# Latent attention on one core: four heads of two sequences a step, query rows packed into blocks of 128

## The reference, cut to what matters

```python
def _L0_attn_ref(x, wq_a, q_a_ln_w, wq_b, wkv_a, kv_a_ln_w, wkv_b, wo):
    H, NOPE, ROPE, VD, KVR = 32, 64, 64, 128, 64
    q = _rmsnorm(x @ wq_a.T, q_a_ln_w) @ wq_b.T          # 256 -> 32 heads x 128
    q_nope, q_pe = q[..., :NOPE], q[..., NOPE:]
    ckv, k_pe = split(x @ wkv_a.T)                       # 64 latents + 64 rope, shared by all heads
    k_nope, v = split(_rmsnorm(ckv, kv_a_ln_w) @ wkv_b.T)
    q_pe, k_pe = rope(q_pe), rope(k_pe)
    scores = einsum('bqhd,bkhd->bhqk', [q_nope, q_pe], [k_nope, k_pe]) * softmax_scale
    attn = softmax(where(causal, scores, min))
    return einsum('bhqk,bkhd->bqhd', attn, v) @ wo.T
```

## Time and profile before

| what | value |
|---|---|
| median of 3 runs | 2403.49 us (2399.36 to 2407.38) |
| the profiled execution | 2404.33 us, of which its span is 2402.7 us |
| busy over the span | PE 97%, PEld 85%, DVE 75%, ACT 52%, POOL 51% |
| attention in the span | first scores at 887.6 us, last exp at 1541.0 us |

### The profile page before, as it was taken

One profiled execution on the slowest core, in us unless ns is written; L12 is line 12 of the kernel. 1 busy time (PEld: TensorE's weight loads), 2 busy tenths in 40 slices (PEclk: granted clock), 3 DMA queues, 4 the chain that ended last, 5 costly groups with the idle time before them and its releaser, 6 DMA issues. The chain is left out here.

```text
span 2402.7 us, 45878 instructions
## 1 busy us (share of the span) xinstructions
PE 2321.9 (97%) x14640; PEld 2038.0 (85%) x14640; DVE 1812.4 (75%) x3575; ACT 1241.6 (52%) x3742; POOL 1216.4 (51%) x1012
## 2 busy tenths in 40 slices
PE   8999999998999979999999999899999998999998
PEld 6888888887677758999999999788888887999998
DVE  8987775896577758888988888655786566777775
ACT  5566654552455549999999999623223223111110
POOL 5567786672133347767776776420675553111110
PEclk9999999999999979999999999899999999999999
DMA  7774567779477720111111112296888997111111
GB/s 249 240 230 149 174 226 254 256 248 323 140 228 241 239 87 24 58 53 56 40 56 52 48 48 74 79 332 188 247 249 236 304 279 262 54 71 71 70 70 53
DMA packets 319400, 382.00 MB, mean 159 GB/s; under 512 B 23680, under 2 KB 227968, under 8 KB 319104
## 3 DMA queue, kind: packets, MB, share of 16 engines
q1 hardware_dynamic: 311472, 352.30, 46.2%
q0 software_dynamic: 7184, 25.69, 2.7%
q10 hardware_dynamic: 576, 2.10, 0.3%
HBM read 297.68 MB, written 81.80 MB: 158 GB/s over the span
## 5 line engine op out<-in xcount | busy, mean ns | idle before, releaser
L1547 ACT ACTIVATE attn_prob<-attn_prob,attn_bias 94x94 f32<-94x94 f32 x1024 | 366.8, 361 | 47.3 <-DVE attn_bias L1623 45.9
L682 DVE TENSOR_TENSOR up_t_lo<-early_raw,up_t_hi 128x512 fp32r<-128x512 f32 (+1 forms) x210 | 220.4, 1054 | 102.1 <-ACT up_t_hi L609 99.1
L551 POOL TENSOR_TENSOR early_raw<-early_raw 128x512 f32<-128x512 f32 (+1 forms) x150 | 222.6, 1488 | 131.1 <-DVE up_t_lo L682 68.2
L1668 POOL TENSOR_TENSOR attn_prob<-attn_prob,attn_share 94x752 f32<-94x752 f32 x128 | 188.1, 1469 | 177.8 <-DVE attn_share L1631 177.8
L1926 POOL TENSOR_TENSOR early_raw<-early_raw 128x512 f32<-128x512 f32 x120 | 171.1, 1431 | 196.1 <-DMA early_raw<-o_t 195.6
L1978 DVE TENSOR_TENSOR out_t_lo<-early_raw,out_t_hi 128x512 fp32r<-128x512 f32 x168 | 162.5, 971 | 133.0 <-ACT out_t_hi L1940 131.8
L1940 ACT ACTIVATE out_t_hi<-early_raw 128x512 fp32r<-128x512 f32 x168 | 105.0, 631 | 302.2 <-POOL early_raw L1926 155.3
L609 ACT ACTIVATE up_t_hi<-early_raw 128x512 fp32r<-128x512 f32 (+1 forms) x210 | 130.5, 622 | 238.7 <-POOL early_raw L551 124.9
L746 PE MATMUL up_ps<-up_t_lo,early_s_hi 128*128 128x512 f32 (+1 forms) x616 | 239.7, 389 | 8.8 <-DVE up_t_lo L682 8.8
L747 PE MATMUL up_ps<-up_t_hi,early_s_lo 128*128 128x512 f32 (+1 forms) x616 | 238.2, 387 | 0.0
L748 PE MATMUL up_ps<-up_t_hi,early_s_hi 128*128 128x512 f32 (+1 forms) x616 | 238.2, 387 | 0.0
(11 more groups left out here) (271 smaller groups left out, 6614.3 us busy)
## 6 DMA issues: line engine op xcount, KB each, us to landing
early_raw<-o_t SPq DMA_DIRECT2D x288, 256.0 KB, 5.0
early_raw<-x_f SPq DMA_DIRECT2D x240, 256.0 KB, 3.7
shared_ring<-w SPq DMA_DIRECT2D x120, 256.0 KB, 4.1
early_raw<-x_f SPq DMA_DIRECT2D x120, 240.0 KB, 3.7
shared_ring<-wvo SPq DMA_DIRECT2D x96, 256.0 KB, 4.9
o_t<-attn_o_t SPq DMA_DIRECT2D x128, 188.0 KB, 1.9
shared_ring<-wo SPq DMA_DIRECT2D x32, 512.0 KB, 6.5
y<-early_raw POOLq DMA_DIRECT2D x24, 512.0 KB, 3.7
```

Source lines behind the costliest of these rows:

```text
L551: nc.gpsimd.tensor_tensor(both[n % 2][:, 0:w], a, b, SEVEN[i].op_b).then_inc(both_done, 1)
L682: nc.vector.tensor_tensor(t_lo[s % NT][:, 0:w], src, t_hi[s % NT][:, 0:w], ALU.subtract).then_inc(lo_done, 1)
L1547: last = nc.scalar.activation(prob[u % NPR][0:SEQ, h, part], prob[u % NPR][0:SEQ, h, part], ACT.Exp, bias=bias[u % 2][0:SEQ, n:n + 1], sca ...
L1668: nc.gpsimd.tensor_tensor(p4, p4, share[u % 2][0:SEQ, :].unsqueeze(2).broadcast_to((SEQ, 8, SEQ)), ALU.mult).then_inc(prob_done, 1)
```

## The change

- An item is still two heads of four sequences at depth 0. From the scores on, a step takes four heads (two items of depth 0, one quad) of two sequences. The 4 x 94 = 376 query rows of a sequence stand in one row of the new buffer `q` and are cut into three blocks of 128 rows (the third reaches 8 rows into the next sequence or into padding). So a step has 6 score matmuls (128 rows by 94 keys) where there were 8, 6 exps of 128 x 94, a mask of 128 x 564, 6 transposes, and 2 matmuls of 376 columns for the weighed values where there were 8 pairs of halves (16 matmuls for two items).
- All four heads use `k_t`; `k_tb` and its two copies are gone. ACT and DVE write the second head's halves to the other partitions.
- `ps_l` has two banks (PE waits for the latents of two items back). `ps_o` has one instead of two, and PE weighs the values of one item at every step. DVE's copy of `ps_o` is first in a step, and its depth is one behind that of the weighed values.
- Depths: D_S 1 to 2, D_N 2 to 3, D_T 4 to 5, D_V (7, 6) to 6, D_O 8 to 7. The unrolled body has 32 steps where it had 16.
- The output of a step is stored with four DMAs (64 x 2 x 94 each, in pieces of 94 floats) where it was one of 128 x 376.
- Weights are split for two pairs of heads (four banks `w_hi`, `w_lo`), one half of a split at every third step, where it was two steps in a row.

```diff
+TILES_Q = -(-GT // P)
+NQ, WQ = 2 * TILES_Q, TILES_Q * SEQ
...
-        k_tb = mem.sb("k_tb", [P, TOK])
+        q = [mem.sb(f"q{i}", [P, 4 * P * TILES_Q]) for i in range(2)]
+        prob = [mem.sb(f"prob{i}", [P, 2, WQ]) for i in range(NPR)]
-        ps_l = mem.ps("ps_l", [P, 512])
+        ps_l = [mem.ps(f"ps_l{i}", [P, 512]) for i in range(2)]
-        ps_o = [mem.ps(f"ps_o{i}", [P, 512]) for i in range(2)]
+        ps_o = mem.ps("ps_o", [P, 512])
...
-        U = 2 * GROUPS
-        D_S, D_N, D_T, D_O = 1, 2, 4, 8
-        D_V = (7, 6)
+        QUAD = 2 * GROUPS
+        U = 2 * QUAD
+        D_S, D_N, D_T, D_V, D_O = 2, 3, 5, 6, 7
...
+        def rows(u, heads):
+            a = q[u // 2 % 2][:, 0:GB * GT].rearrange("p (b h s) -> p b h s", b=GB, h=GB)
+            return a[heads, :, :, :]
...
-                    sp.dma_start(d["o_t"][:, 2 * kb + u // GROUPS, GT * g:GT * g + GT],
-                                 o_t[u % 2][:]).then_inc(o_stored[u % 2], 16)
+                    for c in range(2):
+                        at = GT * (u % QUAD // 2) + SEQ * (2 * (u % 2) + c)
+                        for n in range(2):
+                            sp.dma_start(d["o_t"][64 * n:64 * n + 64, bass.ds(4 * kb + 2 * (u // QUAD), 2), at:at + SEQ],
+                                         o_t[u % 2][64 * c:64 * c + 64, :].rearrange("p (i n s) -> p i n s", i=2, n=2)
+                                         [:, :, n, :]).then_inc(o_stored[u % 2], 16)
...
-                        if not first(j, 1):
-                            pe.wait_ge(free, j)
+                        if ps is ps_r:
+                            if not first(j, 1):
+                                pe.wait_ge(swap_done, j)
+                        elif not first(j, 2):
+                            pe.wait_ge(latent_done, j - 1)
...
-                    for h, (q, keys) in enumerate(((q_a[u % 2], k_t), (q_b[u % 2], k_tb))):
-                        for b in range(GB):
-                            at = GT * g + SEQ * b
-                            last = nc.tensor.matmul(ps_s[0:SEQ, h, SEQ * b:SEQ * b + SEQ], q[:, SEQ * b:SEQ * b + SEQ],
-                                                    keys[:, at:at + SEQ], start=True, stop=True)
+                    ready = j + (2 - u % 2)
+                    pe.wait_ge(latent_done, ready)
+                    pe.wait_ge(rope_a_done, ready)
+                    pe.wait_ge(rope_b_done, ready)
+                    for c in range(2):
+                        b = 2 * (u % 2) + c
+                        at = GT * (u % QUAD // 2) + SEQ * b
+                        for n in range(TILES_Q):
+                            last = nc.tensor.matmul(ps_s[:, c, SEQ * n:SEQ * n + SEQ],
+                                                    q[u // 2 % 2][:, GT * b + P * n:GT * b + P * n + P],
+                                                    k_t[:, at:at + SEQ], start=True, stop=True)
...
-                for back in D_V if m % 2 == 1 else ():
-                    s = stage(k, m, back, U, N)
...
+                s = stage(k, m, D_V, U, N)
...
+                    if not first(j, 1):
+                        pe.wait_ge(o_done, j)
+                    for c in range(2):
+                        b = GB * (u % QUAD // 2) + 2 * (u % 2) + c
+                        last = nc.tensor.matmul(ps_o[64 * c:64 * c + 64, 0:GT], v[0:96, b, :],
+                                                prob_t[u % NPT][0:96, c, 0:GT], start=True, stop=True)
...
-                nc.scalar.activation(k_tb[64:P, :], k_t[0:64, 0:TOK], ACT.Copy).then_inc(keys_done, 1)
...
-                    for h in range(2):
-                        for b in range(GB):
...
+                    for n in range(NQ):
+                        part = prob[u % NPR][:, n // TILES_Q, SEQ * (n % TILES_Q):SEQ * (n % TILES_Q) + SEQ]
+                        last = nc.scalar.activation(part, part, ACT.Exp, bias=bias[u % 2][:, n:n + 1], scale=SCALE,
+                                                    accum_out=total[u % 2][:, n:n + 1])
...
-                        nc.vector.tensor_copy(k_tb[0:64, :], k_t[64:P, 0:TOK]).then_inc(keys_done, 1)
```

More of the change, by code:

```diff
@@ L1316, in attention @@
         sin = mem.sb("sin", [P, GT])
-        k_tb = mem.sb("k_tb", [P, TOK])
+        w_hi += [mem.sb(f"w_hi{i}", [P, 2, 2 * P], F32R) for i in range(2, 4)]
+        w_lo += [mem.sb(f"w_lo{i}", [P, 2, 2 * P], F32R) for i in range(2, 4)]
+        NPR = 4
+        NPT = 4
+        q = [mem.sb(f"q{i}", [P, 4 * P * TILES_Q]) for i in range(2)]
+        prob_t = [mem.sb(f"prob_t{i}", [P, 2, TILES_Q * P]) for i in range(NPT)]
         v = mem.sb("v", [P, BATCH, KR])
-        mask = mem.sb("mask", [P, SEQ])
         swap = [p ^ 1 for p in range(32)]
-        q_a = [mem.sb(f"q_a{i}", [P, GT]) for i in range(2)]
-        q_b = [mem.sb(f"q_b{i}", [P, GT]) for i in range(2)]
         by_cos = mem.sb("by_cos", [P, GT])
@@ L1560, in _, with split @@
             nc.vector.memset(v[64:P], 0.0).then_inc(zeroed, 1)
-            def split(w, p, c):
-                dve.wait_ge(w_hi_done, 2 * p + (c + 1))
-                nc.vector.tensor_tensor(w_lo[w][:, c, :], w_raw[w][:, c, :], w_hi[w][:, c, :],
+            def split(new, w, n, c):
+                dve.wait_ge(w_hi_done, 4 * new + (2 * n + c + 1))
+                nc.vector.tensor_tensor(w_lo[2 * w + n][:, c, :], w_raw[n][:, c, :], w_hi[2 * w + n][:, c, :],
                                         ALU.subtract).then_inc(w_lo_done, 1)
-            split(0, 0, 0)
-            split(0, 0, 1)
+            for n in range(2):
+                split(0, 0, n, 0)
+                split(0, 0, n, 1)
             dve.wait_ge(table_in, 48)
             def body(k, m):
+                s = stage(k, m, D_O, U, N)
+                if s is not None:
+                    j, u, kb = s
+                    dve.wait_ge(weighed, j + 1)
+                    if not first(j, 2):
+                        dve.wait_ge(o_stored[u % 2], 64 * bodied(0, kb, u, 2))
+                    nc.vector.tensor_copy(o_t[u % 2][:], ps_o[:, 0:GT]).then_inc(o_done, 1)
                 s = stage(k, m, 0, U, N)
@@ L1580, in body @@
                     nc.vector.stream_shuffle(swapped[:], ps_r[:, 0:GT], swap).then_inc(swap_done, 1)
-                    if first(j, 1):
-                        nc.vector.tensor_copy(k_tb[0:64, :], k_t[64:P, 0:TOK]).then_inc(keys_done, 1)
-                    for c in range(2):
-                        s = weights_of(k, m, PREP + 1 + c)
-                        if s is not None:
-                            p, w, kb = s
-                            split(w, p, c)
-                s = stage(k, m, D_O, U, N)
-                if s is not None:
-                    j, u, kb = s
-                    dve.wait_ge(weighed, j + 1)
-                    if not first(j, 2):
-                        dve.wait_ge(o_stored[u % 2], 16 * bodied(0, kb, u, 2))
-                    nc.vector.tensor_copy(o_t[u % 2][:], ps_o[u % 2][:, 0:GT]).then_inc(o_done, 1)
+                    s = split_of(k, m, 1)
+                    if s is not None:
+                        new, w, kb, n, c = s
+                        split(new, w, n, c)
                 s = stage(k, m, D_S, U, N)
@@ L1642, in _ @@
             nc.gpsimd.memset(zero[:], 0.0).then_inc(cleared, 1)
+            for n in range(2):
+                nc.gpsimd.memset(q[n][:, GB * GT:], 0.0).then_inc(padded, 1)
             pool.wait_ge(cleared, NPT + 1)
@@ L2436 @@
     q, key = np.arange(SEQ)[:, None], np.arange(SEQ)[None, :]
-    mask = np.zeros((P, SEQ), f32)
-    mask[:SEQ] = np.where(key <= q, 0.0, MASKED)
+    mask = np.zeros((TILES_Q * P, SEQ), f32)
+    mask[:GT] = np.tile(np.where(key <= q, 0.0, MASKED), (GB, 1))
+    mask = np.ascontiguousarray(mask.reshape(TILES_Q, P, SEQ).transpose(1, 0, 2).reshape(P, WQ))
     i, j = np.arange(NR)[:, None], np.arange(NR)[None, :]
```

172 lines of the change are left out of this document (80 added, 92 removed).

## The result

The changed kernel takes 2388.47 us (median of 12 runs, 2382.78 to 2395.83), the one before 2402.64 us in the same comparison (12 runs, 2396.75 to 2407.38). The ratio is 0.9944, with a 95% interval of 0.9932 to 0.9956: 14 us faster. The forecast was 2387. The profiled execution of the changed kernel takes 2390.94 us, with a span of 2389.3, against 2404.33 and 2402.7.

What follows compares the result with a forecast made beforehand. PE was taken as the bound, within 4% of its own work. Steady part 124 x (5.03 - 5.11) = -10, start -5, end -2: about -17 us from 2404.3, so 2387 us, range 2360 to 2412.

Steps and rivals of the forecast that it cites:

- The key reading: Attention step before the change: 5.11 us, of which 4.89 PE's own work and 0.22 waits, 27 us in all.
- Scores: PE's score matmuls: twelve weight loads of 128 columns at 0.11 us, 1.32 us a step; packing saves PE nothing.
- Transposes: PE's six transposes a step: 0.74 us every time, since the weighed values now follow at every step.
- weighed values: PE's group of four instructions of 376 columns an item: 0.77 us, modelled on `tok_down`, upper end 0.82.
- The rival of the halves that don't run side by side: Weighed values on PE: 1.10 us instead of 0.77, 42 us slower, 2429 us; slower side's chance 0.14.
- The way in and out of the weighed values: PE's switch into and out of them at every step: 0.14 us more a step, in the transposes ahead.
- The waits at nothing: PE's waits in the steady part, 0.22 us a step before, were taken as zero after the change.
- DVE's cover: DVE's spare time a step, 0.9 us; once gone, every tenth of a microsecond a step costs 12 us.
- Start: Ahead of the first scores: ACT's key copy wait of 3.09 us and DVE's 1.72 us copy go, about -5 us.
- End: End of attention: +3 for depth, one more us of stores, -6 for the last burst, fewer exps; net -2 us.
- the stores: Four issues on SP at 0.33 us each, 1.3 us a step: hidden in the steady part, +1.0 us at the end.

Runs made afterwards that it cites:

- bursts: Changed kernel with the weighed values of two items together at every second step, two banks for them and one for the latents: 2370.06 us, ratio 0.9860.
- two exps: Changed kernel with two more exps of 128 x 94 in each step, into a spare buffer: 2390.77 us, ratio 0.9945.
- a bank: Changed kernel with one bank for the latents instead of two: 2387.89 us, ratio 0.9930.
- the two runs on weights and keys: Changed kernel's score matmuls with 94 instead of 128 weight columns, 2352.17 us; separately with 47 instead of 94 moving keys, 2385.91 us.
- banks-only run: Kernel before, eight exps kept, with two latent banks, one `ps_o` bank, weighed values at every step and DVE's copy first: 2393.61 us, ratio 0.9960.

## Why the prediction was right

The time, 2387 against 2388.5, and the mechanism were right; that the two times are as near as 1.5 us is partly luck, as the sum below shows. Its steps:

*The key reading*, PE within 4% of its own bound at 4.89 + 0.22: right. (Of the 27 us of waits PE's own rows hold 17.4; the 32 of the prediction are those of the weight loads.) With eight exps or six, PE is at 100 in the windows, and only what changes PE's own sequence moves the changed kernel by more than some 6 us (94 columns of weights -41, bursts -19, against two exps +4, a bank 0, one store -2 and no loop -6).

*Scores* 1.32, measured 1.31. The weight loads around the matmuls of one column had shown the right side, and the two runs on weights and keys confirm it. The Trainium skill ("TensorE: Matmul & The Clock Gate", section "LDWEIGHTS (loading the stationary operand)") gives a load its columns divided by 1.2 in ns, which is an estimate of 1.28 us for the twelve. The trace agrees within 0.03.

*Transposes* 0.74 and *weighed values* 0.77: measured 0.74 and 0.78. The rival of the halves that don't run side by side (1.10) is out, and the two matmuls of `tok_down` were the right model.

*The way in and out of the weighed values*, 0.14 a step: right. Undone by bursts it gives back 0.17 for the transposes (0.74 to 0.57) and 0.15 for the joined groups (1.56 to 1.41) in a pair of steps, and 0.02 where the rope half follows transposes (1225.32 to 1227.48, 2.16): 0.34 a pair, 0.17 a step.

*The waits at nothing*: right, 3.3 us of gaps at the loop's jump aside, which are not waits. These I had not seen: they and the clock after them make the average step 5.03 instead of 5.01. I had taken 5.03 as a midpoint between 5.01 and 5.06, so that the steady part came out at -9.1 against -10 is luck in 0.02 us a step, some 2.5 us in all: the length was right for a reason that I had not named. DVE's cover was right by two errors that cancel: half a split, priced at 1.77 us, took 0.41, and the addition into `q`, not priced, took 0.91 in the middle where that into `q_b` took 0.54. DVE is 84% busy, with 82 foreseen.

*Start* -5, measured -6.4 (first rope matmul to step 3). The 3.09 us of wait for the copied keys went as foreseen. The first scores themselves are no earlier, 887.5 against 887.6: a third step of rope and latents now goes ahead of them.

*End* -2, measured +0.1. This is the term that was mis-sized, and in it the stores: I priced an issue by that of the plain 128 x 376 store, 0.33 us. The new ones:

```profile
L1434 SPq DMA_DIRECT2D o_t<-attn_o_t x512: 595/603/1600, 909.4 to 1539.1; - x171
```

Each takes 0.60. Four after the last copy end at 1539.7, and +1.0 becomes +2.8 by the run with one store. The rest of the end isn't taken apart; in the run with one bank, with the same four stores, it takes 27.6 instead of 28.9. In the steady part the 2.4 us a step hide behind PE's 5.0, as argued.

The sum was 0.9 too good in the steady part and 2.1 at the end, 1.4 too careful at the start, and the two unchanged parts took 2 us more than in the profile of before: -13.4 against -17 in the profiled executions, -14.2 in the medians.

One thing the prediction did not separate: it named banks, depth and fewer exps together as what ends the waits. The runs show that the banks and places alone do, that fewer exps alone nearly end the waits for the latents, and that the waits for DVE's copy go with its place behind the splits. The prediction named the splits as a risk of the change, but not as what made the 14 waits ahead of the weighed values before it.

## What to carry to other kernels

Split the step of the engine nearest its bound into own work and waits before costing a change: here an edit on ACT worth 90 us of busy time could return only the 27 us of waits, and an arrangement with more slack returned them without it. Packing rows into full blocks saves instructions and other engines' time, but it saved TensorE nothing here, where the packed side is loaded as weights and fewer columns move than are loaded: count the columns loaded. Look at what stands ahead of the instruction that frees a buffer, in the order of its engine: a long instruction there is paid by the engine that waits. Groups that use half of the array are cheaper in bursts, since each way in and out cost about 0.15 us here; and what is idle elsewhere after a change is best spent on letting the bound engine's sequence become shorter. Price a small DMA by its own shape: its issue counts too where a store is last.

## What was not expected of the hardware

- The issue of a store of 64 x 2 x 94 in pieces of 94 floats takes SP 0.60 us where 128 x 376 takes 0.33, though it moves a quarter of the bytes; the single store of 128 x 2 x 188 takes 0.37. Landing hardly differs: 2.0 us in the middle, 1.9 before.
- At the jumps back of a body of 32 steps PE starts 1.6 us late, twice. DVE is 3.1 us late at the first jump and not at the second, and behind the second the granted clock drops, too.
- The subtraction of a split on DVE (128 x 256), 1786 ns in the middle before, takes 407 ns now; the row of all 32:

```profile
L1586 DVE TENSOR_TENSOR attn_w_lo<-attn_w_raw,attn_w_hi x32: 400/407/659, 876.8 to 1430.6; 128x256 fp32r<-128x256 f32 x32
```

In the kernel before the two at the start took 420 and 425 ns; the other 30 took 1.67 us or more, and each of these spans a whole multiplication by the sines on POOL (L1655, 0.98 us) and parts of the instructions on both sides of it. In the banks-only run the same splits, at another moment of POOL's step, take 466 in the middle and overlap some 0.3 us of it, but for one of 1857 that again spans the whole. So the length goes with what POOL does beside them, and not with the packing; how the two engines hold each other up no run tests. It is 1.4 us of DVE for each half of a split. In the changed kernel that is not on PE's path. In the kernel before it was, 14 times, through the copy that stood behind the split.
